# Moving an attention mask from TensorE to VectorE, and issuing the down products of an expert layer one chunk later

## The reference

```python
x = x + tanh(g_xattn[0]) * L0_xattn(layernorm(x), ctx, ...)   # 8 experts, top 2 by ctx, relu
x = x + tanh(g_ffn[0])   * L0_ffn(layernorm(x), ...)          # 4 experts, all computed, top 2 gates
x = x + tanh(g_xattn[1]) * L1_xattn(layernorm(x), ctx, ctx, mask, ...)   # 16 heads of 8
x = x + tanh(g_ffn[1])   * L1_ffn(layernorm(x), ...)          # 4-bit quantised gated MLP, width 352
```

```python
h = silu(einsum('td,edf->etf', xf, w1)) * einsum('td,edf->etf', xf, w3)    # 4 experts, f = 512
out = einsum('te,etd->td', gates, einsum('etf,efd->etd', h, w2))

scores = einsum('bhqd,bhkd->bhqk', q, k) / sqrt(8)
scores = where(mask[:, None, :, :] == 0, -1e9, scores)
attn = einsum('bhqk,bhkd->bhqd', softmax(scores), v)
```

## Time and profile before

| what | value |
|---|---|
| median of 3 runs | 1242.68 us (1236.83 to 1244.21) |
| the profiled execution | 1233.73 us, its span 1232.0 us |
| mean granted TensorE clock | 0.897 of full speed |
| PE busy | 981.5 us (80% of the span), 5276 matmuls |
| DVE busy | 753.5 us (61%), 1764 instructions |
| ACT busy | 626.4 us (51%) |
| POOL busy | 581.1 us (47%) |
| DMA | 24.4% of 16 engines for the main queue, most of it before 350 us |

### The profile page before, as it was taken

How to read it: one execution, slowest core, us unless ns; L and a number is a source line. 1 busy time by engine, 2 the same in 40 slices (tenths; PEclk the granted TensorE clock), 3 DMA queues, 4 the chain that set the end, 5 groups by cost and what they waited for, 6 DMA issues and landing times.

```text
span 1232.0 us, 17588 instructions
## 1 busy us (share of the span) xinstructions
PE 981.5 (80%) x5276; PEld 698.8 (57%) x5276; DVE 753.5 (61%) x1764; ACT 626.4 (51%) x1875; POOL 581.1 (47%) x637
## 2 busy tenths in 40 slices
PE   6340799992886997988889798888878888988883
PEld 6220688881654665665566566556655655655551
DVE  3525467563584785776588577657857767654232
ACT  2631466561343765555555565655655656654440
POOL 2477433334555356537345563734555453541213
PEclk9965799996998999979898998998999999997676
DMA  9799577652501001021002102100210200210000
GB/s 276 241 369 343 181 278 264 241 198 59 61 1 28 7 5 37 5 37 26 15 9 31 37 6 37 28 13 10 31 37 5 37 10 6 33 12 12 7 5 5
DMA packets 126513, 93.66 MB, mean 76 GB/s; under 512 B 77546, under 2 KB 105684, under 8 KB 121684
## 3 DMA queue, kind: packets, MB, share of 16 engines
q1 hardware_dynamic: 121268, 82.05, 24.4%
q0 software_dynamic: 4096, 8.40, 2.5%
q10 hardware_dynamic: 1056, 2.10, 0.6%
HBM read 59.46 MB, written 33.06 MB: 75 GB/s over the span
## 4 chain that ended last, share of the span: by engine, by line
PE 44%; POOL 22%; DVE 12%; issue 10%; ACT 9%; DMA 2%; SPq 0%; POOLq 0%; DVEq 0%; ACTq 0%
ACT pr L769 6%; PE U L1124 5%; POOL xs_dram L516 5%; POOL yg L568 4%; PE M L1329 4%; PE U L1128 4%; PE U L1125 4%; POOL h_lo L577 4%; PE M L1335 4%; PE M L1362 3%; DVE xin L967 3%; PE Y L1128 2%; PE M L1326 2%; PE M L1374 2%; PE Y L1124 2%
## 5 line engine op out<-in xcount | busy, mean ns | idle before, releaser
L577 POOL TENSOR_TENSOR h_lo<-h,h_hi 128x512 fp32r<-128x512 f32 x128 | 164.9, 1288 | 237.4 <-ACT h_hi L740 237.1
L769 ACT ACTIVATE pr<-M,nmax 128x128 f32<-128x128 f32 x512 | 180.7, 370 | 51.6 <-DVE nmax L1063 51.4
L734 ACT ACTIVATE h<-U 128x512 f32<-128x512 f32 x128 | 76.4, 597 | 135.5 <-PE U L1128 135.2
L1063 DVE TENSOR_REDUCE nmax<-M 128x4 f32<-128x512 f32 x128 | 87.4, 682 | 86.9 <-PE M L1329 86.3
L1124 PE MATMUL U<-xn_hi,w_hi 128*128 128x512 f32 x256 | 125.3, 489 | 8.1 <-DVE h L1012 6.4
L1008 DVE SCALAR_TENSOR_TENSOR h<-h,U 128x512 f32<-128x512 f32 x128 | 87.5, 683 | 64.2 <-ACT h L734 64.0
L1335 PE MATMUL M<-ident,pr 128*128 128x128 f32 x512 | 84.2, 290 | 42.3 <-ACT pr L769 42.2
L1125 PE MATMUL U<-xn_hi,w_lo 128*128 128x512 f32 x256 | 107.5, 420 | 0.0
L1128 PE MATMUL U<-xn_lo,w_hi 128*128 128x512 f32 x256 | 107.4, 420 | 0.0
L769 ACT ACTIVATION_READ_ACCUMULATOR pr<-M,nmax 128x1 f32 x512 | 107.3, 210 | 0.0
L740 ACT ACTIVATE h_hi<-h 128x512 fp32r<-128x512 f32 x128 | 81.5, 637 | 48.8 <-DVE h L1012 46.7
(11 more groups left out here) (309 smaller groups left out, 2346.7 us busy)
## 6 DMA issues: line engine op xcount, KB each, us to landing
wt<-w_dram SPq DMA_DIRECT2D x23, 1024.0 KB, 4.7
w_dram<-wt SPq DMA_DIRECT2D x8, 1024.0 KB, 8.3
xs_dram<-xr SPq DMA_DIRECT2D x1, 5888.0 KB, 19.7
ys_dram<-acc SPq DMA_DIRECT2D x12, 256.0 KB, 2.3
key_stack<-k_dram SPq DMA_DIRECT2D x48, 64.0 KB
wt<-k_dram SPq DMA_DIRECT2D x48, 64.0 KB
ys_dram<-part SPq DMA_DIRECT2D x11, 256.0 KB, 2.1
pr<-in_L_xattn_W SPq DMA_DIRECT2D x8, 256.0 KB, 6.2
```

Source lines behind the costliest of these rows:

```text
L577: nc.gpsimd.tensor_tensor(h_lo[i % 4][:, :], h32[i % 3][:, :], h_hi[i % 4][:, :].bitcast(fp32), ALU.subtract).then_inc(lo_done, 1)
L769: done = nc.scalar.activation(pr[i % 2][:, c], bank[:, c], ACT.Exp, bias=nmax[i % 4][:, r:r + 1], accum_out=rsum[b % 2][:, HB * r + j:HB * ...
L1063: nc.vector.tensor_reduce(nmax[i % 4][:, :], m_bank(("s", i))[0][:, :].rearrange("p (h k) -> p h k", h=HB), AX.X, ALU.max, negate=True).th ...
```

## The change

Two things. First, the mask product of the `s` step is gone and each score product starts its own sum. DVE's `max` step is now four instructions, one a head: each adds `mneg` to the 128x128 scores in the bank, writes them back to the bank, and gives the row minimum. For this, queries are scaled by the negative of what they were, the mask is +2^100, and `exp` has the scale -1.0, so that the minimum of the negated scores is the bias. `mneg` is plain fp32. The wait for `mask_made` moves from PE's `s` to DVE's `max`, and the `mask` step waits for `nmax_done` of an earlier sequence.

Second, `later` adds 6.0 to the due time of `down`, and of `combine` and `acc` of the first three experts of a group. On PE, `down` of chunk n stands behind `up` of chunk n+2. The last chunk but one of a group gets 3.0, the last nothing.

```diff
-MASKED = -2.0 ** 100
+MASKED = 2.0 ** 100
+LAG1 = 6.0
+def later(what, i):
+
+    if what == "down" and i % N1 < N1 - 2 or what in ("combine", "acc") and i % E1 < E1 - 1:
+        return LAG1
+    return LAG1 / 2 if what == "down" and i % N1 == N1 - 2 else 0
...
-    timed = [(PLACED.get((what, i), t), what, i) for t, what, i in timed]
+    timed = [(PLACED.get((what, i), t + later(what, i)), what, i) for t, what, i in timed]
...
-        mneg = [sb(f"mneg{i}", [P, S], fp32r) for i in range(2)]
+        mneg = [sb(f"mneg{i}", [P, S]) for i in range(2)]
...
-            for w, dst, scale in ((0, WqT, DK ** -0.5), (1, WkT, 1.0)):
+            for w, dst, scale in ((0, WqT, -DK ** -0.5), (1, WkT, 1.0)):
...
-                        done = nc.scalar.activation(pr[i % 2][:, c], bank[:, c], ACT.Exp, bias=nmax[i % 4][:, r:r + 1], accum_out=...)
+                        done = nc.scalar.activation(pr[i % 2][:, c], bank[:, c], ACT.Exp, bias=nmax[i % 4][:, r:r + 1], scale=-1.0, accum_out=...)
...
                     if i >= 2:
-                        dve.wait_ge(m_full, m_at["s", (i - 1) * HB - 1] + 1)
+                        dve.wait_ge(nmax_done, (i - 1) * HB)
...
-                    nc.vector.tensor_reduce(nmax[i % 4][:, :], m_bank(("s", i))[0][:, :].rearrange("p (h k) -> p h k", h=HB), AX.X, ALU.max, negate=True).then_inc(nmax_done, 1)
+                    if i % HB == 0:
+                        dve.wait_ge(mask_made, i // HB + 1)
+                    bank = m_bank(("s", i))[0]
+                    for r in range(HB):
+                        c = slice(r * S, (r + 1) * S)
+                        ins = nc.vector.tensor_tensor_reduce(bank[:, c], bank[:, c], mneg[i // HB % 2][:, :], 1.0, BIG, ALU.add, ALU.min, nmax[i % 4][:, r:r + 1])
+                    ins.then_inc(nmax_done, 1)
...
                     if j == 0:
-                        pe.wait_ge(mask_made, b + 1)
...
-                    nc.tensor.matmul(bank[:, :], ident_r[:, :], mneg[b % 2][:, :].unsqueeze(1).broadcast_to([P, HB, S]), start=True, stop=False)
                     rows = slice(32 * j, 32 * j + STK)
                     for h in range(HB):
-                        ins = nc.tensor.matmul(..., start=False, stop=(h == HB - 1))
+                        ins = nc.tensor.matmul(..., start=True, stop=True)
```

More of the change, by code:

```diff
@@ L631, in _ @@
             nc.scalar.activation(qk_turn[:, 0, :].rearrange("a (j d i) -> a i j d", j=HB, d=DK), qk_rows[:, 0, :].rearrange("a (i j d) -> a i j d", i=HB, j=HB),
-                                 ACT.Copy, scale=DK ** -0.5)
+                                 ACT.Copy, scale=-DK ** -0.5)
             nc.scalar.activation(qk_turn[:, 1, :].rearrange("a (j d i) -> a i j d", j=HB, d=DK), qk_rows[:, 1, :].rearrange("a (i j d) -> a i j d", i=HB, j=HB),
@@ L768, in _ @@
                         c = slice(r * S, (r + 1) * S)
-                        done = nc.scalar.activation(pr[i % 2][:, c], bank[:, c], ACT.Exp, bias=nmax[i % 4][:, r:r + 1], accum_out=rsum[b % 2][:, HB * r + j:HB * r + j + 1])
+                        done = nc.scalar.activation(pr[i % 2][:, c], bank[:, c], ACT.Exp, bias=nmax[i % 4][:, r:r + 1], scale=-1.0, accum_out=rsum[b % 2][:, HB * r + j:HB * r + j + 1])
                     done.then_inc(emptied, 1)
@@ L1325, in _ @@
                         pe.wait_ge(k_loaded[g % 2], 16 * 12 * (g // 2 + 1))
-                    nc.tensor.matmul(bank[:, :], ident_r[:, :], mneg[b % 2][:, :].unsqueeze(1).broadcast_to([P, HB, S]), start=True, stop=False)
                     rows = slice(32 * j, 32 * j + STK)
                     for h in range(HB):
-                        ins = nc.tensor.matmul(bank[:, h * S:(h + 1) * S], qst[g % 2][rows, h, t], kst[g % 2][rows, h, t], start=False, stop=(h == HB - 1))
+                        ins = nc.tensor.matmul(bank[:, h * S:(h + 1) * S], qst[g % 2][rows, h, t], kst[g % 2][rows, h, t], start=True, stop=True)
                     ins.then_inc(m_full, 1)
```

## The result

The changed kernel takes 1224.47 us (median of 4 runs, 1223.23 to 1226.03) against 1242.65 us for the kernel before (median of 4 beside it): ratio 0.9863 [0.9829, 0.9897]. The median of the changed kernel repeats itself within 2 us; it is the kernel before that moves. So the change is worth 0.6 to 1.4%, some 7 to 18 us. I had forecast 1221 us, which is close, and a gain of 22 us, which is more than there is.

The account below looks back on a forecast made before the run. PE, busy 631 of 730 us, was taken as the fullest engine. Won 59.3 less lost 37.3, net 22, takes 1233.73 to 1211.7 us; the profiled run lies 9 under the median, so 1221, 8-in-10 range 1190 to 1258.

Parts of the forecast that it names:

- The mask product: On PE, its removal wins 0.41 us a quad: 32.8 us in the main stretch, bounds 25.8 to 45.1.
- the same 80 quads: Main-stretch quads credited with the mask gain: 63 where PE ends last, 17 of the 47 where the exponentials do.
- The maximum: On DVE, four instructions cost 0.56 us more a quad (bounds 0.18 to 1.32): 26.3 us lost in 47 quads.
- The first rival: VectorE becomes the bound: from 0.90 us more a quad the change loses; at 1.32, 1270 us. Chance 0.16.
- Down later, the waits: PE's waits for h_lo end: 6.5 us won in the head, three quarters of 26.4, 20.0, in the main stretch.
- the next limit: Group 0's MoE: gate products following one another through tanh and gated lie just behind; all 6.5 us still won.
- Moves on POOL and DVE: combine ahead of mix costs 5 us, acc between POOL's steps of f_x 3 us; together 8 us lost.
- The tail: Last 18 quads: mask product and maximum share one chain, 0.56 less 0.41 added each, 3 us lost.
- The wait that moves: Main stretch: every stall at down reappears at pt, 20 of the 22 us are gone, 1241 us. Chance 0.18.
- The falling clock: Tail: without the mask columns about ten quads more run at TensorE's lower clock, 11 us lost, 1232. Chance 0.10.
- the signs I had named: Signs of a wrong forecast: pt waiting in far more than 47 quads, f_xt's wait grown, tail clock far below 0.73.
- the 63 quads: Main-stretch quads where PE ends last; their slack hides the dearer maximum, which would otherwise cost 35 us more.

Follow-up runs that it names:

- e1: Changed kernel with the lag set to 0.0, so the mask part alone, without the later down products: 1229.83 us, ratio 0.9951 to the kernel before.
- e2: Kernel before with only the later down, combine and acc; mask product and single maximum stay: 1229.95 us, ratio 0.9933.
- e5: Changed kernel, unedited, timed a second time: 1225.93 us against 1234.49 for the kernel before, ratio 0.9943.
- e11: Changed kernel with only acc of the third expert due 4.0 later, behind POOL's third step of f_x: 1202.44 us, ratio 0.9737.
- e6: Changed kernel with combine of the first and third expert due 1.5 later and acc of the third 4.0 later: 1210.38 us, ratio 0.9802.
- e12: Kernel before with the later down products, and combine and acc moved out of the chain of f_x: 1220.14 us, ratio 0.9869.
- e7: Changed kernel with mix cut into two steps of four instructions, a maximum, gated and swiglu between them: 1210.69 us, ratio 0.9787.
- e10: Kernel before with mix cut into two steps and nothing else: 1219.2 us against 1236.24, ratio 0.9856.
- e3: Changed kernel with one 128x512 reduction instead of four instructions, the mask left out of the computation: 1213.34 us, ratio 0.9796.

## Why the prediction came out as it did

The forecast time was hit with a net gain that was too large: against the profiled execution 22 us were forecast and 8.6 came. That it was hit is in part luck: the median I started from, 1242.68, was at the upper end of what the kernel before takes (1234.49 to 1242.65 in the four sets of runs), and two prices that were too high cancel. The two parts of the change bring 6 to 8 us (e1) and 8 us (e2), and these add up to about the whole. Step by step:

**The mask product** (32.8 us in the main stretch, 7.4 in the tail): the mechanism was right, the size at least twice too large. The start-to-start time of 0.41 us was read as the product's price. PE's busy time says 0.19 to 0.26 a product, the time from `pt` to score product 0.21; with 0.21 the same 80 quads give 17 us, under my lower bound of 25.8. The runs give 5 to 17 us in all. What the step overlooked is that the weight load behind it is not drawn forward when it goes.

**The maximum** (26.3 us, and 18 times 0.56 in the tail): right in kind, too dear. The quad is 0.34 us longer, within my bounds of 0.18 to 1.32. I had taken operation plus a pipelined read from ACT's pair, 0.29 a head; here the read hides nearly whole, 0.25. (By the figures shown there, four times 0.48 is 1.92 and four times 0.29 is 1.16; that changes the sum by about 1 us.) The Trainium skill's "VectorE: DVE Perf Modes", section "The TRN2 errata", gave an estimated 0.38 us more, which this trace supports; I should have gone by it rather than by ACT. The Trainium skill's word that an accumulator output makes a second instruction (the same page, section "Two Vector instructions with no wait between them") is seen too, at 140 ns busy. The runs give 6 to 18 us. The first rival (DVE the bound) needed 0.90 us more and is out; in e1, where the two terms are by themselves, they come to plus 6 to 8 us, my 40.2 less 36.4 to plus 4: both prices were at least twice too high, and the errors cancel.

**Down later, the waits.** Right that the wait for h_lo ends: 26.4 us to nothing in the main stretch, 6.5 to 0.6 in the head. Wrong about what is kept. In the main stretch three quarters were to be kept; e2 shows 19 us of new waiting at `f_xt` and `nxT`, and the second of these I had not named. In the head the gain was 6.5 by forecast; `back` comes 0.9 us earlier (4.3 in e5). The head's first transposes start 0.8 us later than before in after and 1.0 earlier in e5, so counted from there it is 1.7 and 3.3 us shorter. PE in the head of after, the chunk behind `mix`:

```profile
340.91 0.60 PE L1277 MATMUL M<-ident,gates 128*128 128x128 f32 x4
345.00 0.80 PE L1138 MATMUL U<-xn_hi,w_hi 128*128 128x512 f32 x1 [3.49 <-DVE h L1016]
```

and the windows of that place, after and then before:

```profile
341.00:345.00 4.00, 0.51 (x6) 0.27 (x4) 3.90 (x9) 0.60 (x1) 1.64 (x2) 0.89 0.00 0
345.00:357.00 12.00, 12.00 (x49) 9.90 (x50) 10.02 (x27) 4.99 (x9) 5.73 (x6) 0.75 0.01 2
```

```profile
341.00:345.00 4.00, 2.10 (x11) 1.27 (x10) 3.90 (x10) 1.12 (x2) 1.25 (x1) 1.00 0.00 0
345.00:357.00 12.00, 9.99 (x47) 6.96 (x48) 9.63 (x27) 4.65 (x8) 7.55 (x7) 1.00 0.01 2
```

PE is done with what it has 1.7 us sooner (345.00 less 3.49 is 341.5; before, the gate product of that place starts at 344.87 after a wait of 1.63, so from 343.2) and waits that much longer for a release that comes no sooner. Most of what it had won since the head's start is given back at one place, and the clock is 0.75 for the 12 us behind it (0.86 in e5), where it had been 1.00. I had called the gate chain the next limit and not asked where `mix` stands in it.

**Moves on POOL and DVE** (3 us for `acc`, 5 for `combine`): this step was the furthest off. `acc` costs each `f_xt` that it precedes 0.71 us, as I had 0.65, but that agreement is luck: I had half of its 1.3 us hold POOL up, and the trace has POOL ready 0.63 us before it may go on. It is DVE's `gd`, slower beside `acc`, that makes `x_m` late. The waits are now 13 and not 9, and most of their length is `combine`'s, which I had not put there (20.0 us with `acc` moved, 4.4 with both). And what I had left out is TensorE's clock, for which the sum has no term in the main stretch: moving `acc` away (e11) gains 1.3 to 2.1%, 15 to 25 us, where the wait shortened by 5.3 and PE's idle time by nothing; PE's busy time fell by 20.1 us at 0.97 for 0.93. That the gain in e11 is the clock's is shown by these counts. That `f_xt`'s wait is what had lowered it is argued from four places of after and not shown; the rows of the kernel before, e6 and e12 named above speak against a simple rule. The 5 us for `combine` ahead of `mix` weren't isolated: e6 and e11 leave that one where it is, and e7 with e10 only say that `mix` is dear in both kernels.

**The tail** (3 us): it is 4.6 us longer in the profile, but not by the sum's terms. In e1, which has the mask product gone and the four instructions without the lag, the tail is 133.8 us, 1.1 less than before: `pt` waits 5.0 us longer and PE is busy 5.5 us less. After has 5.2 us more of PE's busy time than e1 for the same products, at a clock of 0.69 for 0.73. What lowers the clock there is open: e3 and e6, with the lag in them too, have 0.73. After's own tail is 139.5 us in both of its profiled executions; the others were profiled once.

**The rivals.** The wait that moves looked right in the rows (`pt` took on 21.3 us of the 26.4), but e2 shows only 4.2 of it with the lag alone; the rest came with the mask part, and the lag's waits moved to `f_xt` and `nxT`. Nor does the time follow it: e3, with the cheap maximum, still waits 42.3 us at `pt`, 10 more than before, and is 24.5 us faster than before. The falling clock came true in part, in the head, a little in the main stretch (0.94 to 0.93, 0.92 in e5) and in the tail, where it costs 5 us by e1. But e1 has no mask product either and keeps 0.73 there, so the missing columns, which I had named, aren't the cause. Of the signs I had named, `f_xt`'s wait grown, `pt` waiting in more quads and a tail clock under 0.73 all showed; the 63 quads do have the slack that I read from few of them, since the four instructions cost 6 to 18 us in all, where 128 times 0.34 would be 44.

## What to carry to other kernels

Price a removed product by what its successor's start gains (its weight load may not move up), not by the distance to the next row. When steps are moved later, list for every engine which chain they now stand in; here moving one POOL instruction of 1.3 us gained 15 to 25 us (e11). Ask too which DVE instructions with two inputs in SBUF will then run beside it. And count a wait of TensorE not by its length alone: look at the granted clock of the 10 us behind it, and compare busy time for the same number of matmuls before putting a gain down to a wait.

## What the runs showed of the hardware

A DVE operation of 128x4, `gd`, whose two inputs are in SBUF, takes 0.17 us in e11 and 0.86 us in after, where it falls beside POOL's `acc` (the rows stand with e11). There it ends within 0.03 us of `acc`'s end (646.13 and 646.11 us), and so in all six pairs. It stands ahead of `x_m` in DVE's order, so `acc` delayed `f_x` through DVE, while POOL itself was ready. The same is seen in `mix`, whose inputs are also both in SBUF: one of its instructions takes 339 ns in the group of e7's second half, and 994 on average in the first half, which runs beside POOL's `lo` and `acc`.

```profile
L974 DVE SCALAR_TENSOR_TENSOR xin<-yg,gwA,xin 128x128 f32<-128x128 f32 x32 | 29.9, 994 | 13.7 <-DMA yg<-ys_dram,slot 13.7
L981 DVE SCALAR_TENSOR_TENSOR xin<-yg,gwA,xin 128x128 f32<-128x128 f32 x32 | 9.0, 339 | 0.0
```

In the kernel before, the first `mix`, with no POOL instruction beside it, takes 2.31 us for all eight, against 6.07 in the earlier trace rows:

```profile
299.19 2.31 DVE L967 SCALAR_TENSOR_TENSOR xin<-yg,gwA,xin 128x128 f32<-128x128 f32 x8 [13.90 <-DMA yg<-ys_dram,slot]
```

The Trainium skill, "SBUF — State Buffer", section "Who interferes with whom", says that a DVE instruction with two SBUF inputs contends with a GpSimd instruction that reads SBUF; the rows agree.
